# A perceiver layer's loops written out, and their separate semaphore increments taken out

## The reference

```python
x = x + xattn(layernorm(x), ctx_1024)   # x (16, 64, 256); context (16, 1601, 128)
x = x + attn(layernorm(x))              # 16 heads of 16; q, k, v rounded to fp8 with one scale each
x = x + ffn(layernorm(x))               # "ffn": gates choose one of 16 heads for k and v; causal attention
```

## Time and profile before

| | |
|---|---|
| median of 3 runs | 1466.46 us (1465.87 to 1466.65) |
| profiled execution | 1466.3 us, its span 1464.5 us |
| mean granted TensorE clock | 0.976 |
| busy: PE, DVE, ACT, POOL | 1377.9, 1262.4, 1196.8, 1059.2 us (94, 86, 82, 72% of the span) |
| queries, cross loop, straight rest of the cross stage, self-attention | about 0 to 125, 190 to 1144, 1144 to 1302, 1302 to 1464 us |
| instruction fetch | queue q14: 175 packets, 1.43 MB; queue q8: 20 packets, 0.33 MB |

### The profile page before, as it was taken

How to read it: one execution, slowest core, us unless ns; L and a number is a source line. 1 busy time by engine, 2 the same in 40 slices (tenths; PEclk the granted TensorE clock), 3 DMA queues, 4 the chain that set the end, 5 groups by cost and what they waited for, 6 DMA issues and landing times. The chain is left out here.

```text
span 1464.5 us, 31654 instructions
## 1 busy us (share of the span) xinstructions
PE 1377.9 (94%) x5980; PEld 934.4 (64%) x5980; DVE 1262.4 (86%) x5010; ACT 1196.8 (82%) x4845; POOL 1059.2 (72%) x1583
## 2 busy tenths in 40 slices
PE   6997999999999999999999999999999998957886
PEld 4774666666666666666666666666666666845554
DVE  6998889898998899898989899998899898766894
ACT  5897898889888988889888889898988887435673
POOL 5886889888988888898889888988888884000000
PEclk9998999999999999999999999999999999977997
DMA  3000000000000000000000000000000001000000
GB/s 138 0 23 24 1 24 2 24 3 24 1 23 2 23 2 23 11 14 22 2 25 0 24 2 24 1 23 2 24 11 17 23 30 65 1 1 1 8 11 12
DMA packets 10211, 25.25 MB, mean 17 GB/s; under 512 B 848, under 2 KB 6640, under 8 KB 9888
## 3 DMA queue, kind: packets, MB, share of 16 engines
q1 hardware_dynamic: 9728, 23.49, 4.4%
q10 hardware_dynamic: 288, 0.00, 0.0%
HBM read 22.44 MB, written 1.05 MB: 16 GB/s over the span
## 5 line engine op out<-in xcount | busy, mean ns | idle before, releaser
L1123 ACT ACTIVATE c_unused<-c_prod 124x128 f32<-124x128 f32 x1664 | 493.0, 298 | 88.2 <-DVE c_prod L1344 81.2
L1657 POOL TENSOR_TENSOR c_acc<-c_acc,c_prob 123x1024 f32<-123x1024 f32 (+1 forms) x192 | 461.9, 2406 | 25.1 <-ACT c_prob L1130 24.5
L1355 DVE CUSTOM_DVE_ANT_0 c_multiplied<-psK,c_c 124x128 f32<-124x128 f32 x1664 | 381.7, 285 | 54.9 <-PE psK L920 54.8
L919 PE MATMUL psK<-wkh,c_cTh 128*124 128x512 f32 x832 | 414.2, 498 | 12.7 <-DVE c_cTl L1383 10.2
L939 PE MATMUL psO<-c_prob,raw 123*128 123x512 f32 (+1 forms) x832 | 392.1, 594 | 0.0
L1344 DVE TENSOR_TENSOR c_prod<-psK,c_c 124x512 f32<-124x512 f32 x416 | 286.2, 688 | 55.7 <-PE psK L920 42.1
L920 PE MATMUL psK<-wkl,c_cTh 128*124 128x512 f32 x832 | 329.4, 396 | 0.0
L1123 ACT ACTIVATION_READ_ACCUMULATOR c_unused<-c_prod 124x1 f32 x1664 | 311.7, 187 | 0.0
L1366 DVE TENSOR_TENSOR c_prob<-psS,c_ss 124x512 f32<-124x512 f32 x416 | 265.9, 681 | 0.5 <-POOL c_ss L1640 0.4
L1130 ACT ACTIVATE c_prob<-c_prob,shift 124x1024 f32<-124x1024 f32 x208 | 236.7, 1138 | 0.0
L919 PEld LDWEIGHTS psK<-wkh,c_cTh 128*124 128x124 f32 x832 | 154.2, 185 | 118.5 <-DVE c_ss L1355 47.8
(11 more groups left out here) (328 smaller groups left out, 2255.9 us busy)
## 6 DMA issues: line engine op xcount, KB each, us to landing
raw<-in_ctx SPq DMA_DIRECT2D x16, 799.5 KB
raw<-in_L_xattn_Wq SPq DMA_DIRECT2D x6, 256.0 KB, 7.7
xs<-in_x SPq DMA_DIRECT2D x4, 256.0 KB, 4.6
big<-in_L_xattn_Wk SPq DMA_DIRECT2D x1, 1024.0 KB, 7.5
c_prod<-in_L_xattn_Wo SPq DMA_DIRECT2D x1, 1024.0 KB, 5.2
out<-s_y SPq DMA_DIRECT2D x8, 128.0 KB, 1.7
big<-in_L_ffn_W_qkv SPq DMA_DIRECT2D x1, 768.0 KB, 11.3
raw<-in_L_xattn_Wv SPq DMA_DIRECT2D x1, 768.0 KB, 4.2
```

What stands on the lines that cost most here:

```text
L919: nc.tensor.matmul(psK[0:ROWS, c % 2, :], cTh[:, slot, :], T.wkh[:, cols], start=True, stop=False)
L1123: last = nc.scalar.activation(unused[:, j, :], prod[:, k % 2, c // 2, j * CD:(j + 1) * CD], ACT.Copy, accum_out=ss[:, k % 2, 0, h:h + 1])
L1355: last = nc.vector.tensor_tensor_reduce(multiplied[:, j, :], psK[0:ROWS, 1, cols], c2[:, k % NT, :], 1.0, 0.0, ALU.mult, ALU.add, ss[:, k ...
L1657: nc.gpsimd.tensor_tensor(acc[0:rows, batch % 2, :], acc[0:rows, batch % 2, :], prob[0:rows, probs(s), :], ALU.add).then_inc(S.acc, 1)
```

## The change

All `Fori` become Python `range`, on all engines and SyncE too; so each turn stands in the stream for itself, and all waits and addresses are constants. The tests for `isinstance(i, int)` go. `alone`, its 12 calls and the two semaphores `passed` go, in the straight steps as well. The order of the instructions on each engine is the same, and so are the operations.

```diff
-def alone(eng, sem):
-
-    eng.sem_inc(sem, 1)
...
 def load_context(nc, sp, T, dram, i, b, sems):
-    one = rows[bass.ds(2 * i + b, 1)] if not isinstance(i, int) else rows[2 * i + b:2 * i + b + 1]
+    one = rows[2 * i + b:2 * i + b + 1]
...
 # cross_attention, pipeline(eng, emit, end, begin)
-            with eng.Fori(0, NPAIR - 1) as i:
+            for i in range(NPAIR - 1):
                 for v in steps(i, False):
                     emit(i, *v)
...
-            n = slice(pair, pair + 1) if isinstance(pair, int) else bass.ds(pair, 1)
+            n = slice(pair, pair + 1)
...
 # cross_attention, SyncE
-            with sp.Fori(0, NPAIR - 1) as i:
+            for i in range(NPAIR - 1):
                 for b in range(2):
                     sp.wait_ge(S.vmm, done(i, NT * (b + 1) - 1, 2))
-                    alone(sp, W.passed)
                     load_context(nc, sp, T, dram, i + 1, b, loaded[b])
...
             def key_rest(i, r):
                 pool.wait_ge(R.scaled, done(i, r, 1))
-                alone(pool, W.passed)
                 nc.gpsimd.tensor_scalar(ss[:, r % 2, 4, :], ss[:, r % 2, 6, :], -0.5, 1.5, ALU.mult, ALU.add).then_inc(R.rest, 1)
...
 # self_attentions, pipeline(eng, step)
-            with eng.Fori(0, NPAIR - 3) as i:
+            for i in range(NPAIR - 3):
                 step(i + 3, i + 2, i + 1, i)
...
 # self_attentions, SyncE
-            with sp.Fori(0, NPAIR) as i:
+            for i in range(NPAIR):
                 sp.wait_ge(G.y, at(i, 2, 2))
-                sp.dma_start(out[bass.ds(i, 1), :, :].rearrange("n p c -> (n p) c"), y[:, :]).then_inc(stored, 16)
+                sp.dma_start(out[i:i + 1, :, :].rearrange("n p c -> (n p) c"), y[:, :]).then_inc(stored, 16)
                 sp.wait_ge(stored, 16 * i + 16)
-                alone(sp, W.passed)
...
-def scores_pe(nc, pe, S, passed, scores, qT, kbd, start=True):
+def scores_pe(nc, pe, S, scores, qT, kbd, start=True):
-    alone(pe, passed)
...
             def moments(f):
                 dve.wait_ge(A.x3, at(f, 1, 1))
-                alone(dve, W.passed)
                 nc.vector.bn_stats(stats[:, :], latents(f)).then_inc(G.stats, 1)
                 dve.wait_ge(G.stats, at(f, 1, 1))
-                alone(dve, W.passed)
                 nc.vector.bn_aggr(mv[:, :], stats[:, :]).then_inc(G.moments, 1)
```

More of the change, by code:

```diff
@@ L803, in more @@
         def more(i, batch):
-            return batch < 2 or not isinstance(i, int) or i < NPAIR - 1
+            return batch < 2 or i < NPAIR - 1
         psM_all, psT_all = psM[:, :], psT[:, :]
         def den_bank(i, batch, half):
-            return psT_all if isinstance(i, int) and (i, batch, half) == (NPAIR - 1, 1, 1) else psM_all
+            return psT_all if (i, batch, half) == (NPAIR - 1, 1, 1) else psM_all
         def steps(i, last):
@@ L840, in late @@
         def late(i, v):
-            return v - (TP - 4) if isinstance(i, int) and i == LAST and v is not None and v >= TP - 4 else None
+            return v - (TP - 4) if i == LAST and v is not None and v >= TP - 4 else None
         def out_half(i, batch, half):
@@ L1317, in evacuate @@
                 act.wait_ge(S.ql, batch_done(i, batch, 2))
-                alone(act, W.passed)
                 nc.scalar.activation(out_half(i, batch, 0), psO[:, 0, :], ACT.Copy).then_inc(S.oev_a, 1)
@@ L1779, in latents @@
         def latents(i):
-            n = slice(i, i + 1) if isinstance(i, int) else bass.ds(i, 1)
+            n = slice(i, i + 1)
             return T.xs[:, n, :].rearrange("p n c -> p (n c)")
@@ L1829, in attention_scores @@
                 pe.wait_ge(AS.pTe, at(a, NC, 0))
-                scores_pe(nc, pe, AS, W.passed, att_scores, q8T, lambda c: k8bd[:, c, :, :])
+                scores_pe(nc, pe, AS, att_scores, q8T, lambda c: k8bd[:, c, :, :])
             def turn_output(a):
@@ L1875, in feed_scores @@
                 pe.wait_ge(G.krep, at(f, 1, 1))
-                alone(pe, W.passed)
                 for r in range(2):
@@ L1882, in feed_scores @@
                 pe.wait_ge(G.kbd, at(f, 1, 1))
-                scores_pe(nc, pe, GS, W.passed, ffn_scores, q2T, lambda c: k2bd[:, :, :], False)
+                scores_pe(nc, pe, GS, ffn_scores, q2T, lambda c: k2bd[:, :, :], False)
             def duplicate_selected(f):
@@ L1932, in scaled @@
                 act.wait_ge(A.q8, at(a, 1, 0))
-                n = slice(a, a + 1) if isinstance(a, int) else bass.ds(a, 1)
+                n = slice(a, a + 1)
                 for part in range(3):
@@ L2213, in build @@
         T = Shared()
-        T.cross, T.later = signals(nc, ctx, ("wc", "loaded00 loaded01 loaded10 loaded11 passed " + HEAD_SEMS + " " + OUT_SEMS), ("main", MAIN_SEMS), ("keyrms", KEY_SEMS))
+        T.cross, T.later = signals(nc, ctx, ("wc", "loaded00 loaded01 loaded10 loaded11 " + HEAD_SEMS + " " + OUT_SEMS), ("main", MAIN_SEMS), ("keyrms", KEY_SEMS))
         T.ident, T.identb = sb("ident", [P, P]), sb("identb", [P, P], BF16)
@@ L2231, in build @@
                 queries(nc, T, psum, dram)
-                T.self, T.later = signals(nc, ctx, ("ws", "found swept sc blocks stored passed"), ("att", ATT_SEMS), ("attsm", SM_SEMS),
+                T.self, T.later = signals(nc, ctx, ("ws", "found swept sc blocks stored"), ("att", ATT_SEMS), ("attsm", SM_SEMS),
                                           ("ffn", FFN_SEMS), ("ffnsm", SM_SEMS), ("ffnln", ROOT))
```

## The result

The changed kernel took 1450.13 us, the median of 4 runs (1448.55 to 1451.55); the kernel before took 1466.16 us in the same rounds (1465.02 to 1466.65). The ratio is 0.9895, 95% interval 0.9883 to 0.9906. That is 16 us faster where 11.8 were forecast, and 0.4 us under the lower end of the range. The profiled execution took 1451.55 us, its span 1449.8.

What follows compares the result with a forecast made beforehand. TensorE was taken as the bound in the cross-attention loop, mostly VectorE's chain in self-attention. Terms 7.4 + 0.5 + 2.1 + 1.8 = 11.8 us gave 1455 us, with 8 in 10 from 1450.5 to 1461.

Steps and rivals of the forecast that it cites:

- Edges, 7.4 us: Cross-attention loop: writing it out removes six back edges, whose excess over the straight tile spacing of 5.09 us is 7.4 us.
- Waits on registers' values cost TensorE nothing here, and the edges do: Cross-attention loop: an ordinary tile inside a turn takes 5.08 us despite register waits, so only the back edges cost TensorE time.
- GpSimd's increments, 2.1 us: Cross loop, key_rest: without increments GpSimd frees VectorE's L1542 0.3 us sooner at 7 places, so TensorE idles 2.1 us less.
- The increments in moments(), 1.8 us: Self-attention stage: VectorE's two increments cost 0.23 us a pair on the chain of waits, 1.8 us over 8 pairs.
- 0, if TensorE's chain takes over: Lower bound on the gain from removing VectorE's increments in moments(); the upper bound was 2.5 us.
- TensorE's three, taken as nothing: TensorE's three increments in the scores stand behind other matmuls: no gain, bounds 0 and 0.9 us.
- Register waits in the self-attention part, 0.5 us: Self-attention loop, maxima to shift: 1.36 us in the loop, 1.26 in straight steps; 5 turns give 0.5 us.
- B: Rival: code is still fetched once a turn, the 7.4 us stay; 1462 us, or 1466 without the small terms; chance 0.07.
- C: Rival: slower, late code fetches twice or more a turn in straight code; 1473 us at two a turn; chance 0.06.
- D: Rival: another L1542 collides on the shared pair, up to 5.8 us lost instead of 2.1 gained; 1463 us; chance 0.05.
- A: Rival: only the edges gain, time freed by increments is waited away elsewhere; 1459 us; chance 0.20 with its clock variants.
- A sign of being wrong that came true: The forecast is wrong if, among other signs, the stages before and after the loops move by over 1 us.

Runs made afterwards that it cites:

- the four one-engine loops: Kernel before, all loops written out, increments kept, one engine alone keeping its cross loop: VectorE 1462.96, GpSimd 1455.65, TensorE 1452.79, ScalarE 1450.50 us.
- the kernel with one edge: Kernel before, its cross loop made one straight turn and a loop of two turns with three copies each, increments kept: 1460.13 us, ratio 0.9950.

## Why the prediction was right, and where not

The kernel gained 16.0 us where 11.8 were forecast. Of the forecast's terms 7.9 us (edges, register waits in the self-attention part) came as described; 2.1 came at the forecast place from another cause, which is luck; 1.8 did not come; and 3.4 (positions 11 and 13) stood in no term.

- **Edges, 7.4 us: right in size and place.** Six edges, 37.95 - 30.42 = 7.5 us. That it is VectorE's gap and no other's, the forecast only hinted at with the earlier trace rows; the four one-engine loops show it (7.1 of it with VectorE alone).
- **"Waits on registers' values cost TensorE nothing here, and the edges do": the step that failed.** From an ordinary tile (5.08 us), where VectorE and GpSimd wait for TensorE and any delay of theirs is covered, it was concluded that inside the turns the loops cost nothing. In the tiles with extra work they do. GpSimd's loop alone costs 2.9 us, with no edge in it, and VectorE's adds 0.6 at position 11 and 0.6 at position 24 (38.10 - 37.52 and 38.53 - 37.88), and 2.2 at position 13. About registers the step was mostly right: the larger part goes with short stops at fixed places of the bodies, which the kernel with one edge doesn't have at the same register arithmetic.
- **GpSimd's increments, 2.1 us: the place and the size right, the cause wrong.** GpSimd's operation starts 0.4 us sooner in relation to VectorE's, which falls to 1.1 us, as described. But with the increments and without the loop this is so as well, and in the changed kernel they cost nothing. What made GpSimd late was mostly its 0.25 us stop in position 20; that the three increments' 0.3 us are much the same size is luck. All increments of the cross part together: 0.6 us.
- **Position 13, 2.3 us: in no term.** 5.40 against 5.08 stood in the starts of before and was not looked at; the forecast compared two ordinary tiles with the edges. It goes with the place of VectorE's code.
- **The increments in moments(), 1.8 us: wrong, 0.** The gaps were there and closed (0.15 to 0.03), but the chain waits for TensorE's scores behind them. The bound "0, if TensorE's chain takes over" was the case. TensorE's three, taken as nothing, are among those that cost 0.09 us a step.
- **Register waits in the self-attention part, 0.5 us: 5 x 0.13 = 0.65.** The gain of the stage, 2.3 us in the forecast, is 1.8 by the medians with and without (1451.22 - 1449.41) and 2.4 by this profile: much the forecast sum, from other terms. The 2.4 holds differences of the clock as well: the last stage of six kernels with one and the same self-attention part (loops out, increments kept) runs from 252.0 to 257.4 us. The six steps between the last seven statistics, most of them at full clock, give 92.0 - 90.5 = 1.5 us.
- **The rivals.** B and C fell: no gap without a releaser of over 0.3 us is left on VectorE or GpSimd in straight code. D fell: no other L1534 is over 1.12 us. A was too small, but what it said of the increments, that the freed time is waited away elsewhere, is what the runs show.
- **A sign of being wrong that came true.** The stage before the loop moved by 1.85 us, over the 1 us that the forecast allowed; it is the clock's, as shown above.

By the terms as measured: edges 7.5, position 13 2.3 (37.81 - 35.46), positions 11 and 24 3.9 (79.05 - 75.17, the increments' part among them), self-attention 1.5 to 2.4. That makes 15.2 to 16.1, where the medians say 16.0.

## What to carry to other kernels

Read a rate from every tile of a loop, not from an ordinary one: what costs nothing where an engine has slack is paid in the few tiles where it has none, and those repeat each turn. A gap of 2 us in a profile is worth what the bounding engine waits for it; three engines had the same gap here, and one was paid for. Small gaps count too if they come once a turn in a stretch without slack: 0.25 us on GpSimd cost TensorE 0.3 us three tiles later. And a gap that closes in the trace is no gain until the wait behind it is looked at.

## What the runs showed of the hardware

- What a loop's edge costs differs by engine and body. TensorE alone looped cost 0.11 us at an edge (5.18 against 5.07), while VectorE, GpSimd and ScalarE each stood still for 1.4 to 2.0 us. With three copies in the body of every engine TensorE itself stood still for 3.04 us. Whether the length of the body decides is not shown; no run varies it on one engine alone.
- Loop bodies had short stops far from the branch, at the same instruction in each of seven turns: GpSimd 0.25 to 0.27 us, and VectorE some 0.33 us (its gap 0.67 against 0.33).
- 33 instructions more ahead of a loop, at a place where they cost nothing, made the loop 1.7 us faster in 7 turns, by 0.33 us at one instruction of each turn. Kernels with loops can differ by as much for no reason in their text.
- An instruction that only increments, between two waits on constants, costs 0.11 to 0.12 us on its own engine (GpSimd 0.20 against 0.08, VectorE 0.14 against 0.03), and mostly nothing in the time.
- Where a 128x512 operation of VectorE on two operands in SBUF met one of GpSimd that had started first, it ended 0.54 to 0.55 us behind GpSimd's in three rows: it took 1.52, 1.44 and 1.10 us for starts 0.03, 0.11 and 0.45 us behind, and 0.69 with no such operation beside it.
